# Fifth layer of a graph network: its ring holds high and low parts side by side, and VectorE adds the low half of the product to the biased residual rows and then the high half

## What is computed

```python
def _sage_conv(x, src, dst, Wl, b, Wr):
    agg = jax.ops.segment_sum(x[src], dst, num_segments=n)
    cnt = jax.ops.segment_sum(jnp.ones((src.shape[0],), x.dtype), dst, num_segments=n)
    mean = agg / jnp.maximum(cnt, 1.0)[:, None]
    return mean @ Wl + b + x @ Wr

x = _layernorm(x + _L0_gnn_ref(x, ...))     # two layers,   128 -> 128 -> 128
x = _layernorm(x + _L1_gnn_ref(x, ...))     # three layers, 128 -> 256 -> 256 -> 128
```

## Time and profile before

| | us |
|---|---|
| median of three runs | 4938.33 (4938.22 to 4954.48) |
| the profiled execution, its own time | 4940.29 |
| its span from first to last instruction | 4938.2 |
| PE busy | 4735.3 (96%) |
| DVE busy | 3532.4 (72%) |
| ACT busy | 2601.5 (53%) |
| POOL busy | 2279.1 (46%) |

### The profile page before, as it was taken

The page is one execution under the profiler, slowest core; times in us unless marked ns, Lnnn a source line. Parts: engine busy times, 40 slices in busy tenths (PEclk is TensorE's granted clock), DMA queues, the critical chain, the costliest instruction groups (busy, mean ns, idle before and its releaser), DMA issues. The chain is left out here.

```text
span 4938.2 us, 149021 instructions
## 1 busy us (share of the span) xinstructions
PE 4735.3 (96%) x40046; PEld 4631.6 (94%) x40047; DVE 3532.4 (72%) x9770; ACT 2601.5 (53%) x7279; POOL 2279.1 (46%) x2182
## 2 busy tenths in 40 slices
PE   1999989999989999999899999999999999999999
PEld 1899979999989999999899999999999999999999
DVE  4788858888879999998566666666666455555555
ACT  1555558888874444443333333333332667766776
POOL 2777755555534444442422222222221655555653
PEclk9999989999989999999999999999999999999999
DMA  1788868888866666666555555555555777777776
GB/s 41 209 237 235 237 187 242 241 243 242 241 191 204 207 207 207 206 207 198 172 179 176 176 179 176 176 179 175 177 179 160 218 237 237 234 236 236 237 236 201
DMA packets 1247144, 1007.16 MB, mean 204 GB/s; under 512 B 69988, under 2 KB 1177857, under 8 KB 1247046
## 3 DMA queue, kind: packets, MB, share of 16 engines
q1 hardware_dynamic: 1170442, 824.83, 54.7%
q0 software_dynamic: 75712, 180.66, 12.7%
q10 hardware_dynamic: 892, 0.40, 0.0%
HBM read 645.48 MB, written 360.13 MB: 204 GB/s over the span
## 5 line engine op out<-in xcount | busy, mean ns | idle before, releaser
L1256 POOL DMA_INDIRECT f_e_rows_b<-g,f_e_idx_b x392 | 392.5, 1001 | 1046.9 <-ACT f_e_idx_b L1375 978.1
L1395 ACT ACTIVATE f_ring_b<-f_e_product_b,t_rec_all 128x256 f32 (+1 forms) x784 | 329.5, 471 | 832.8 <-PE f_e_product_b L1350 832.8
L1322 PE MATMUL f_product_b<-b_r_all,f_t_hi_b 128*128 128x256 f32 x2352 | 724.7, 308 | 0.6 <-DVE f_onehot_b L1438 0.5
L1390 ACT ACTIVATE f_t_hi_b<-f_turned_b 128x512 fp32r<-128x512 f32 x588 | 330.6, 597 | 645.6 <-PE f_turned_b L1293 645.4
L1326 PE MATMUL f_product_b<-b_r_all,f_t_lo_b 128*128 128x256 f32 x2352 | 660.8, 281 | 0.0
L1324 PE MATMUL f_product_b<-b_r_all,f_t_hi_b 128*128 128x256 f32 x2352 | 660.2, 281 | 0.0
L1430 DVE SCALAR_TENSOR_TENSOR f_t_lo_b<-f_turned_b,f_t_hi_b 128x512 fp32r<-128x512 f32 x588 | 388.2, 688 | 369.9 <-ACT f_t_hi_b L1390 369.9
L755 POOL DMA_INDIRECT m_e_rows_b<-g,m_e_idx_b x392 | 398.5, 1017 | 495.2 <-ACT m_e_idx_b L903 426.2
L1329 PE MATMUL f_product_b<-f_ring_b,f_onehot_b 128*128 x3136 | 622.5, 279 | 0.0
L1256 POOL DMA_INDIRECT f_e_rows_b<-x,f_e_idx_b x392 | 392.2, 1000 | 496.1 <-ACT f_e_idx_b L1375 425.5
L999 DVE TENSOR_TENSOR m_onehot_b<-iota_all,t_win_all 128x512 f32<-128x512 f32 (+1 forms) x392 | 252.7, 645 | 477.0 <-PE m_product_b L864 477.0
(11 more groups left out here) (208 smaller groups left out, 12360.3 us busy)
## 6 DMA issues: line engine op xcount, KB each, us to landing
g<-f_rows_out_b SPq DMA_DIRECT2D x392, 512.0 KB
f_rows_in_b<-g SPq DMA_DIRECT2D x196, 512.0 KB
m_rows_in_b<-g SPq DMA_DIRECT2D x196, 512.0 KB
m_t_full_a<-in_x_flat_dram SPq DMA_DIRECT2D x196, 256.0 KB
h<-m_rows_out_a SPq DMA_DIRECT2D x196, 256.0 KB
m_rows_in_a<-h SPq DMA_DIRECT2D x196, 256.0 KB
m_res_in_a<-in_x_dram SPq DMA_DIRECT2D x196, 256.0 KB
x<-m_rows_out_a SPq DMA_DIRECT2D x196, 256.0 KB
```

Of the source, the lines that this page charges most:

```text
L1256: pool.indirect_dma_start(e_rows[:, s, a, :], None, h, bass.IndirectOffsetOnAxis(ap=e_idx[:, s, a:a + 1], axis=0), bounds_check=bound, oob ...
L1322: pe.matmul(to, t_hi[:, s, k, cols], cv["r2"][:, k, 0, :], start=(t % per == 0 and k == 0), stop=False, skip_group_check=True)
```

## The change

b3 is now built with `split=True`, beside `biased=True`, which it had:

- The ring's slots are 256 columns wide and float32r: high part by ScalarE as before, low part by two VectorE instructions (`ring_low`). One-hot matrices are float32r too. A window is one pass with 256 columns in place of two with 128.
- The product has four pairs of halves in two banks, and two buffers of that: four banks. To fit, `m_e_turned` and `m_e_product` have one buffer each (`EB = 1`). With that come two stricter waits on TensorE: `turn_edges` waits until ScalarE has copied the edge rows of the turn before, and `project` until VectorE has written the ring's low part of the projection before.
- VectorE's step is `step_split`: `ring_low`, the seven one-hot matrices in one instruction, the new `add_low` (low half of the product plus biased residual rows, into `m_res_in`), reciprocal, `add_up` (high half plus that), shift, statistics.
- What went away (`mix`, `normalise_rest`, `shared`, `bare`) was used by no layer. The layers a1, a2, b1 and b2 keep their instructions.

```diff
+    EB = 1 if split and flat is None else 2
...
-        e_turned = [pr.ps(c, f"m_e_turned{i}") for i in range(2)]
-        e_product = [pr.ps(c, f"m_e_product{i}") for i in range(2)]
+        e_turned = [pr.ps(c, f"m_e_turned{i}") for i in range(EB)]
+        e_product = [pr.ps(c, f"m_e_product{i}") for i in range(EB)]
...
                 wait(pe, gathered[s], p.turn(D) + 1)
+                if EB == 1:
+                    wait(pe, s_efull, p.n())
...
-                wait(pe, s_ring, p.n(-1))
+                wait(pe, s_ring, p.n(1 - EB))
...
                     if split:
-                        wait(v, s_part, g.n(1))
-                        v.tensor_tensor(total[:, s, :, :], high, part[:, s, :, :], ALU.add).then_inc(s_sum.sem, 1)
+                        wait(v, s_lower, g.n(1))
+                    elif biased:
+                        wait(v, s_biased, g.n(1))
                     else:
...
+                    v.tensor_tensor(total[:, s, :, :], high, res_in[:, s, :, :], ALU.add).then_inc(s_sum.sem, 1)
...
+            def add_low(g):
+
+                s = g.slot(2)
+                wait(v, s_product, g.n(1))
+                wait(v, s_biased, g.n(1))
+                v.tensor_tensor(res_in[:, s, :, :], halves(s)[:, :, 1, :], res_in[:, s, :, :],
+                                ALU.add).then_inc(s_lower.sem, 1)
...
                 if not is_last(g):
                     compare(g.plus(1), 0, WINDOWS)
+                if norm and has(g, 1):
+                    add_low(g.plus(-1))
+                if norm and has(g, 2):
+                    inverse(g.plus(-2))
                 if has(g, 1):
                     add_up(g.plus(-1))
+                if norm and has(g, 2):
+                    offset(g.plus(-2))
+                if norm and has(g, 1):
+                    moments(g.plus(-1))
+                    aggregate(g.plus(-1))
...
-            dict(name="b3", h=g2, out=o2, relu=True, w=2, f_out=128, turned=False, biased=True, Wl=b_wl3, Wr=b_wr3, b=b_b3,
+            dict(name="b3", h=g2, out=o2, relu=True, w=2, f_out=128, turned=False, split=True, biased=True, Wl=b_wl3, Wr=b_wr3, b=b_b3,
```

More of the change, by code:

```diff
@@ L645, in narrow_pass @@
         ring = pr.sb(c, "m_ring", [P, RING * C * fo], F32R if split else F32)
-        if split:
+        if split and not norm:
             part = pr.sb(c, "m_part", [P, 2, T, fo])
@@ L668, in narrow_pass @@
         names = ("turned", "full", "onehot", "product", "sum", "stats", "meanvar", "std", "rstd", "shift", "normed",
-                 "index", "eturned", "efull", "eproduct", "ring", "ringhi", "part", "mixed", "rest", "biased", "eps")
+                 "index", "eturned", "efull", "eproduct", "ring", "ringhi", "part", "lower", "biased", "eps")
         (s_turned, s_full, s_onehot, s_product, s_sum, s_stats, s_meanvar, s_std, s_rstd, s_shift, s_normed,
-         s_index, s_eturned, s_efull, s_eproduct, s_ring, s_ringhi, s_part, s_mixed,
-         s_rest, s_biased, s_eps) = [pr.counter("m_" + x) for x in names]
+         s_index, s_eturned, s_efull, s_eproduct, s_ring, s_ringhi, s_part, s_lower,
+         s_biased, s_eps) = [pr.counter("m_" + x) for x in names]
         s_done = s_normed if norm else s_sum
-        s_total = s_mixed if split else s_sum
         block = c.enter_context(nc.Block())
@@ L715, in load_res @@
             def load_res(g):
-                wait(sp, s_total, g.n(-1))
+                wait(sp, s_sum, g.n(-1))
                 sp.dma_start(res_in[:, g.slot(2), :, :], view(res, g, P)).then_inc(res_here[g.slot(2)].sem, 16)
@@ L836, in own @@
                 wait(pe, s_sum, g.n(-1))
-                if norm and not split and not biased:
+                if norm and not biased:
                     pe.matmul(product[s][:, :], pr.two_rows[:, :],
@@ L950, in normalise @@
                 wait(act, stored[s], g.turn(2))
-                for t in range(T - shared):
-                    if shared and t == T - shared - 1:
-                        wait(act, s_rest, g.n(1))
+                for t in range(T):
                     ins = act.activation(rows_out[:, s, t, :], total[:, s, t, :], ACT.Identity,
@@ L962, in step @@
                     edges_full(p)
-                if split and has(g, 1):
+                if split and not norm and has(g, 1):
                     low_part(g.plus(-1))
@@ L1041, in moments @@
                 s = g.slot(2)
-                wait(v, s_total, g.n(1))
+                wait(v, s_sum, g.n(1))
                 for t in range(T):
@@ L1064, in offset @@
                                        in1=rstd[:, s, :], op0=ALU.mult, op1=ALU.mult).then_inc(s_shift.sem, 1)
-            def normalise_rest(g):
-                s = g.slot(2)
-                wait(v, s_rstd, g.n(1))
-                wait(v, stored[s], g.turn(2))
-                for t in range(T - shared, T):
-                    ins = v.tensor_scalar(rows_out[:, s, t, :], total[:, s, t, :], mean_var[:, s, t, 0:1],
-                                          rstd[:, s, t:t + 1], ALU.subtract, ALU.mult)
-                ins.then_inc(s_rest.sem, 1)
             def step_split(g, p):
@@ L1106, in step @@
                     compare(g.plus(1), FIRSTS, EXTRAS)
-                if shared and has(g, 2):
-                    normalise_rest(g.plus(-2))
                 if norm and has(g, 1):
@@ L1118, in _ @@
                 offset(At(G - 2))
+            if norm and split:
+                add_low(At(G - 1))
             add_up(At(G - 1))
-            if shared:
-                normalise_rest(At(G - 2))
             if norm:
@@ L1145, in narrow_pass @@
         s_ringhi.passed(G)
-        s_part.passed(G)
-        if norm:
-            s_mixed.passed(G)
-    if shared:
-        s_rest.passed(G)
+        (s_lower if norm else s_part).passed(G)
     if biased:
```

32 lines of the change are left out of this document (7 added, 25 removed).

## The result

The changed kernel takes 4863.73 us (median of 4 runs, 4862.35 to 4866.26), the kernel before 4938.31: ratio 0.9842, 95% interval 0.9821 to 0.9862. It is faster by 74.6 us, where the forecast was 119. The time lies in the range of 4793 to 4870, but above 4852, the upper end of the forecast's own case; 45 us of the gain are missing.

A forecast was written before the change was run, and what follows sets the result against it. TensorE's passes were taken to bound b3. Per step, 0.74 us saved at the windows less 0.13 of holes gives 0.61; over 196 groups 119.6 us, from 4940.3 to 4820.7, set at 4819 us against the median; range 4793 to 4870.

The forecast's parts named there:

- the forecast's own case: Step of b3: TensorE holes of 0 to 0.3 us, taken 0.13, step 4.94; 4793 to 4852 us; chance 0.72.
- (a): TensorE's sequencer becomes the bound, as in a1: 0.53 us lost a step, step 5.34, 4899 us; chance 0.12.
- (c): VectorE's comparison against GpSimd's bias addition: mild, VectorE bound, about 4870 us, chance 0.05; full, 4975 us, chance 0.04.
- windows 0.74 saved: TensorE's seven windows in b3: 14 passes, 1.56 us, become 7 of 256 columns, 0.82 us; saves 0.74 a step.
- The sequencer's lead: At b3's last windows and next transposes: registers come late, costing 0 to 0.3 us a step with late transposes; taken 0.13.
- The edge transposes' wait for ScalarE's copy: TensorE in b3: with one buffer, edge transposes and the number load behind them can come up to 0.3 us late.
- The projection's wait for the ring: TensorE's projection waits for the previous ring's low part: 2.2 us of nearly 4 between projections, so costs nothing.
- Transfers, "No hole": Node rows in b3: 6.1 us from issue to need, 5.4 with all else queued ahead; 265 GB/s; no hole.
- VectorE, 4.46 us at most: VectorE's step in b3 grows from 3.10 to 4.46 us at most, 0.48 under the step of 4.94; costs nothing.
- (b): Transfers set b3's pace: with a ceiling of 242 GB/s the step is 5.41 us, 4911 us; chance 0.05.
- (d): TensorE's windows: a pass of 256 float32r columns costs as much as two of 128; chance 0.02.
- The rule on the sequencer's 62 ns: TensorE's sequencer takes about 62 ns per matmul: 43 passes, 2.7 us, plus 2.4 give a 5.1 us step, 4852 us.

The follow-up runs named there:

- e7: Changed kernel with the edits of e8 and e1 (SyncE's order, numbers loaded early): 4807.29 us, ratio 0.9727 to the kernel before.
- e5: Changed kernel with the edits of e8, e1 and e2 together: 4803.32 us, ratio 0.9714 to the kernel before.
- e10: Changed kernel with SyncE's residual load alone moved (group g+1 in place of g+2), the store left where it was: 5073.62 us, ratio 0.9848 to the kernel before.
- e8: Changed kernel with SyncE's order edited in b3: residual rows of group g+1 in place of g+2, stores one group later: 4817.05 us, ratio 0.9744.
- e1: Changed kernel with TensorE's load of window numbers in b3 ahead of the edge projection: 5072.50 us, ratio 0.9845 to the kernel before.
- e6: Changed kernel with the edits of e8 and e2 (SyncE's order, bias ahead of gathers): 4816.78 us, ratio 0.9743 to the kernel before.
- e2: Changed kernel with GpSimd's bias addition in b3 ahead of its two gathers: 5084.56 us, ratio 0.9870 to the kernel before.
- e11: Kernel before with e8's diff, which takes no effect there, so the kernel before run again: 5150.22 us, ratio 0.9996.

## Why the prediction was right or wrong, point by point

- **The number in the range: in part luck.** The forecast's own case was holes of 0 to 0.3, up to 4852; the holes were 0.32. The range reached to 4870 for rivals (a) and mild (c), neither of which sets the pace. Of the signs named, the step of 5.14 lies outside 4.85 to 5.05, and the comparison lasts 1.52 us, over the 1.2 that was to count against the forecast (it turned out to cost nothing by itself, e7 against e5). The holes at the windows and behind them, longer once in six steps, came as described.
- **What bounds the kernel; windows 0.74 saved: right.** In e7 the last three windows and what follows them are 0.118 to 0.121 apart (0.166 inside them in the changed kernel), and e7's step of 4.82 is the predicted "step without holes", 4.81. e7 lies at 0.9727 x 4938 = 4803; "with no holes" was 4793.
- **The sequencer's lead, 0 to 0.3, taken 0.13: the right place, the wrong size.** The term that was mis-sized is the one that took 807 ns for a slow load, from the two loads of the earlier trace rows. Loads have a mean of 0.92 now and reach 1443, and that alone (e10) makes 0.28 of holes. With loads of 0.60 the lead costs 0.06 (e8), less than the 0.13. The row of before already held the sign: 602 and 807 of one and the same instruction, a spread that I took as given. It hangs on the store: in the trace of before, 84 loads that start 1.3 to 1.5 us behind it have a mean of 0.79, and 42 at 1.5 to 1.7 have 0.61.
- **The edge transposes' wait for ScalarE's copy, up to 0.3 late: not seen.** No wait at L792 stands in the list of the changed kernel. **The projection's wait for the ring, nothing: right**, none in the list.
- **Transfers, "No hole": wrong, hidden behind the first.** The time to spare was right: 6.1 us forecast, 6.0 measured. So was the mean of the transfer: 5.4 us with all else queued ahead, and rows land 5.0 us after their issue in the median. What failed was to call the 0.7 us between them enough: it came from an average rate, and the landing varies from step to step, up to 6.3 us. e1 shows TensorE without its rows at a lead of 5.2 us, e10 without such waits at 7.6.
- **VectorE, 4.46 us at most, costs nothing while its slack lasts: half right.** It is never the bound (741.36 / 156 = 4.75 busy, 5.14 step). But its slack was not free: SyncE issues in order behind its second addition, and node rows stand behind that.
- **Rival (a), the sequencer as the bound, 4899: no.** It costs holes of 0.3 like the upper end of the forecast, not 0.53. **(b), transfers set the pace, 4911: no**, e7 passes 272 GB/s where the case assumed 242 as the ceiling. **(d): no.**
- **Rival (c), VectorE against GpSimd: the mild case happens in nearly every step.** The comparison in one piece, 1084 ns in a1, takes 1518 in b3:

```profile
L985 DVE TENSOR_TENSOR m_onehot_b<-iota_all,t_win_all 128x896 fp32r<-128x896 f32 x156 | 236.7, 1518 | 0.6 <-PE m_product_b L852 0.5
```
```profile
L761 POOL TENSOR_TENSOR m_res_in_b<-m_res_in_b,b_bias_all 128x512 f32<-128x512 f32 x157 | 201.7, 1284 | 8.0 <-DMA m_res_in_b<-x 4.1
```

In 148 of the 156 steps GpSimd's bias addition is under way when the comparison starts, and the comparison lasts 1.08 us plus what is left of the addition less 0.12, with a scatter of 0.006: as if it did nothing until GpSimd is all but done. GpSimd's addition isn't lengthened (1284 ns, 1.28 in the earlier trace rows). By the rule of the Trainium skill, "SBUF — State Buffer" (Who interferes with whom), the two exclude each other for a whole instruction; the trace agrees. e8 against e6, and e7 against e5, price it: with SyncE's order mended, 1.40 to 1.45 us against 1.08 change the step by less than 0.03.
- **The rule on the sequencer's 62 ns: my sum was wrong, and no run decides on the figure.** The step of 5.1 us that I drew from it, 4852 us, is close to the measured 5.14 by accident: e7 issues the same 43 passes and the same registers in 4.82 us with TensorE busy throughout. But the 2.4 us that I added, from the number load to the last register, already hold the window passes that lie between. The Trainium skill, "TensorE: Matmul & The Clock Gate" (What happens when you issue a matmul), gives the 62 ns for a sequencer whose hardware decoding is off, and no trace here shows whether it was. An estimate by that page without the windows counted twice, 36 x 0.062 + 2.4, is 4.6 us, which e7 doesn't exclude.
- **The sum.** Forecast 0.61 x 196 = 119.6; the step gave 0.41 x 196 = 80, and 74.6 were measured. Missing are 0.20 x 196 = 39 us of holes, and some 5 outside the steady part.

## What to carry to other kernels

When a change makes the bounding engine's step shorter, list what is issued in order behind the engines that grow, DMA issues above all: a wait of SyncE for a sum becomes a late load for someone else, two hops away. If removing a suspected cause changes nothing, look whether a second one of the same size stood behind it at the same place, and remove both, before calling the first innocent. The steps of one trace, sorted by the length of the suspected instruction, are a second witness that needs no run. The best version is the changed kernel with e8's SyncE order and an early number load (e5 or e7, ratio 0.971 to 0.973), faster than both kernels.

## What the runs showed of the hardware that I had not expected

- A load of registers from a table by TensorE's sequencer takes 0.59 us when nothing is in its way, and 0.92 in the mean of the changed kernel, up to 1.44 (1.69 in e2), when a 256 KB store was issued 0.5 to 1.7 us ahead of its start; it then ends about 2 us after the store's issue. Why is open. Other issues can fall into that time without harm: in e7 the residual rows go out 1.4 us ahead of the load in the median, in e1 the node rows 1.2 us, and the loads take 0.59 in both. Nor is it the traffic as a whole, at 272 GB/s in e7:

```profile
L811 PEldq TENSOR_LOAD <-t_slot_all x146: 587/592/616, 4000.6 to 4699.5; - x146
```

- That VectorE waits for GpSimd can be read from one line: a comparison whose mean is 1518 ns where its like takes 1084. Its record includes the time in which it is held.
- The kernel before took 4938 to 4941 us on two occasions and 5153 on two others. Layer b3 is alike (step 5.55 in both); a1 is where most of it arises, 166 of the 220 us between the two traces (its last pass starts at 679 us in the kernel before and at 845 in e11, the same program on the other chip). In the 125 to 690 us of e11 TensorE is busy for 460.52 us at a granted clock of 0.92 and 174 GB/s are moved, against 542.66, 0.99 and 227 in the earlier trace rows. Why is open; the ratios of one and the same change were the same on both (0.9842 and 0.9845).

```profile
125.00:690.00 565.00, 460.52 (x3179) 418.48 (x3178) 341.58 (x606) 229.55 (x760) 352.21 (x312) 0.92 0.64 174
```
